# Feed-forward of a vision tower: the next chunk's first gatings ahead of the input's quantisation, products ahead of transposes, mean square on GpSimd

## The chip, the cores and the metric

The kernel runs on one core of one Trainium2 chip. The metric is the time of one execution in microseconds, as the device measures it. The engines are TensorE (PE; its weight loads are PEld), VectorE (DVE), ScalarE (ACT), GpSimd (POOL) and SyncE (SP), which issues DMAs.

## The reference, cut to what matters

A tower of an attention mixer, a gated linear attention, a mixture of experts, a linear attention over channels and, last, a quantised feed-forward on 4 x 3136 tokens of width 192. The change touches the feed-forward alone:

```python
def rmsnorm(x, g):
    return x * jax.lax.rsqrt(jnp.mean(x * x, axis=-1, keepdims=True) + EPS_NORM) * g

def activation_quant(x):
    scale = 127.0 / jnp.maximum(jnp.max(jnp.abs(x), axis=-1, keepdims=True), EPS_Q)
    return jnp.clip(jnp.round(x * scale), -128, 127) / scale

# bitlinear(x, w, g): x_norm = rmsnorm(x, g); quantise x_norm; multiply by w rounded to -1, 0, 1
h = bitlinear(x, w_in, g_in)          # 192 -> 2 x 512
up, gate = jnp.split(h, 2, axis=-1)
y = jax.nn.silu(gate) * up
return bitlinear(y, w_out, g_out)     # 512 -> 192
```

The result is added to the residual.

## The kernel before

The five phases follow one another. In the last one, `attention_and_ffn_phase` (L1651), the 12544 tokens are 28 chunks (`NC`) of 448, each four tiles (`TPC`, q = 0 to 3) of 112 tokens on the partitions. The channel attention runs over the chunks first; then the feed-forward runs over them again, with the channel attention's last map (`map_late`, `add_half`) mixed into its chunks g = 1 to 7. These are called early chunks here, the others middle chunks, apart from the last two.

There is no planner: each engine's program is written out in order, and semaphores (`F[...]`) join them. For chunk g of the feed-forward:

- VectorE: `weigh_in` (input times gain), `largest_in` (maximum), `quant_in` (L2482 to L2493: five small operations on 4 values a partition, each waiting for the one before, then four roundings and a conversion to bf16). `gated(g, q)` (L2501) makes y of tile q as silu times the up product times a scale. `mean_square` (L2506), `largest_y` (L2510, two tiles each), `quant_y` (L2525 to L2537, small operations and half of the rounding), `result` (L2547, output times scale plus residual).
- TensorE: `transpose_in` (L2035), `into(g, q)` (L2048: the gate and the up product of tile q), `transpose_y` (L2060), `outof(g, pair)` (L2081).
- ScalarE: `take_x` (L2224, PSUM to xT), `silu` (L2230), `squares` (L2240, the sum of y squared), `scaled_y` (L2247) and `whole_y` (L2253, the other half of the rounding and the conversion), `take_y` (L2259, PSUM to yT).
- GpSimd: `weigh` (L1872, yg = y times gain, one tile of 112 x 512 each), `root_of` (L1877, mean square to the power of -1/2).
- SyncE stores the chunk.

The loop is skewed: in turn g, chunk g's gatings stand with the input quantisation of chunk g + 1, the input weighing of chunk g + 2, and the output of chunk g - 1. Buffers limit it: y, yg5, xT and yT exist once, the products' PSUM banks and sg twice; `into(g, q)` waits until tile q - 2 is gated. `APART` = 8: input transposes up to chunk 8 share PSUM with those of y.

VectorE's turn g ends with `quant_y(g)`; the next operations in the trace, from L2482 on, are turn g + 1's `quant_in(g + 2)`.

Of the kernel before, what the change touches and what calls it, by code (L numbers as in the profile page):

```python
# [11 lines left out]
ALU = mybir.AluOpType  # L12
# [11 lines left out]
TPC = CH // T  # L24
CPI = TOK // CH
NC = B * CPI
# [17 lines left out]
HID = 256  # L44
# [1606 lines left out]
def attention_and_ffn_phase(nc, ins, h, bns, mean, rstd, var, minus, eye, rows_out, out):  # L1651

    HID = 512
# [7 lines left out]
    with ExitStack() as ctx:  # L1661
# [82 lines left out]
        ssq = sb("ssq5", [T, TPC])  # L1744
# [12 lines left out]
        def pga(g, q):  # L1757
# [9 lines left out]
        names5 = ("w_in", "gin_in", "set", "wc", "wsum_mm", "wsc_out", "ready", "xq_out", "xtr_mm", "xT_out", "in_mm", "up_mm",  # L1767
                  "sg_out", "y_out", "yg_out", "ssq_out", "r2_in", "r2_out", "yq_out", "ytr_mm", "yT_out", "o_mm",
                  "o_out", "stored", "dvec", "dvec2", "xg_out", "am_out", "fac_in", "fac_out", "scaled", "d2_out",
                  "xr_out", "yr_out", "s2_out", "ya_out")  # L1770
        F = {n: sem(f"{n}_5") for n in names5}
        out_t = out.rearrange("b (t p) d -> p (b t) d", p=T)
        first_in = [sem(f"first_in{i}_4") for i in range(4)]
# [31 lines left out]
        @block.gpsimd  # L1805
        def _(pool):
            for n, (buf, value) in enumerate(((eps5[:], 1e-5), (mhalf[:], -0.5), (xTB[RB:RB + 1], 1.0),
                                              (wl[64:128, 1, :].bitcast(F32), 0.0))):
                nc.gpsimd.memset(buf, value).then_inc(S["w_ready"], 1)
                pool.wait_ge(S["w_ready"], n + 1)  # L1810
            nc.gpsimd.memset(ones[:], 1.0).then_inc(F["set"], 1)
            pool.wait_ge(F["set"], 1)
            nc.gpsimd.memset(mhalf5[:], -0.5).then_inc(F["set"], 1)
            pool.wait_ge(F["set"], 2)

            def add_rows(g, k):

                if k:
                    pool.wait_ge(first_in[g % 4], 16 * (g // 4 + 1))
                else:  # L1820
                    pool.wait_ge(S["xa_out"], g + 1)
                r0 = k * NTOK + g * CH
                nc.gpsimd.dma_start(acc[g % 4], rows_out[r0:r0 + CH].rearrange("(q p) d -> p q d", p=T),
                                    accum_op=ALU.add).then_inc((first_in, both_in)[k][g % 4], 16)

            def add_bet(g):

                nc.gpsimd.dma_start(h[:, g * TPC:(g + 1) * TPC, :], bet.unsqueeze(1).broadcast_to([T, TPC, D]),
                                    accum_op=ALU.add).then_inc(bet_in[g % 4], 16)

            def factor(g):

                pool.wait_ge(S["agg_out"], g + 1)
                nc.gpsimd.tensor_tensor(veps[:], agg[:, :, 1], eps5[:], ALU.add).then_inc(S["veps_out"], 1)
                pool.wait_ge(S["veps_out"], g + 1)
                if g >= 1:
                    pool.wait_ge(S["nrm_out"], g)
                nc.gpsimd.tensor_tensor(rst[:], veps[:], mhalf[:], ALU.pow).then_inc(S["rst_out"], 1)

            def factor4(g):  # L1840

                pool.wait_ge(S["agg4_out"], g + 1)
                nc.gpsimd.tensor_tensor(veps4[:], agg4[:, :, 1], eps5[:], ALU.add).then_inc(S["veps4_out"], 1)
                pool.wait_ge(S["veps4_out"], g + 1)
                if g >= 1:
                    pool.wait_ge(S["xn_ready"], g)
                nc.gpsimd.tensor_tensor(rst4[:], veps4[:], mhalf[:], ALU.pow).then_inc(S["rst4_out"], 1)

            pool.wait_ge(S["e_in"], 32)
            for s in range(-LEAD, NC):  # L1850
                if here(s + 5):
                    add_rows(s + 5, 0)
                if here(s + 3):
                    factor(s + 3)
                if here(s + 5):
                    add_bet(s + 5)
                    add_rows(s + 5, 1)
                if here(s + 2):
                    factor4(s + 2)

            def factor5(n, cols):

                pool.wait_ge(F["fac_in"], min(n + 1, 2))
                nc.gpsimd.tensor_tensor(fac[:, cols], var[:, cols], mhalf5[:, cols], ALU.pow).then_inc(F["fac_out"], 1)

            def weigh(g, pair):

                for q in (2 * pair, 2 * pair + 1):
                    if g:
                        pool.wait_ge(F[("ya_out", "yr_out")[pair]], g)  # L1870
                    pool.wait_ge(F["y_out"], g * TPC + q + 1)
                    nc.gpsimd.tensor_tensor(yg5[:, q, :], y[:, q, :], gout[:], ALU.mult).then_inc(F["yg_out"], 1)  # L1872

            def root_of(g):

                pool.wait_ge(F["r2_in"], g + 1)
                nc.gpsimd.tensor_tensor(r2[:], ms2[:], mhalf5[:, 0:TPC], ALU.pow).then_inc(F["r2_out"], 1)  # L1877

            factor5(0, slice(0, HEAD))
            pool.wait_ge(F["gin_in"], 32)  # L1880
            for g in range(NC):
                weigh(g, 0)
                weigh(g, 1)
                root_of(g)
                if g in (AFTER, AFTER + 1):
                    half = HEAD + (g - AFTER) * (NT - HEAD) // 2
                    factor5(1 + g - AFTER, slice(half, half + (NT - HEAD) // 2))

        @block.tensor
        def _(pe):  # L1890
# [230 lines left out]
            into(1, 1)  # L2121
            for g in range(1, NC):
                late = NC - CPI + g - 1
                transpose_y(g - 1)
                if late < NC:
                    into(g, 2)
                    if g + 1 < NC:
                        transpose_in(g + 1)
                else:
                    if g + 1 < NC:  # L2130
                        transpose_in(g + 1)
                    into(g, 2)
                into(g, 3)
                if late < NC:
                    map_late(late, 0)
                outof(g - 1, 0)
                if late < NC:
                    map_late(late, 1)
                outof(g - 1, 1)
                if g + 1 < NC:  # L2140
                    enter(g + 1)
                    into(g + 1, 1)
# [5 lines left out]
        def _(act):  # L2148
# [116 lines left out]
            for g in range(NC):  # L2265
                if g:
                    scaled_y(g - 1)
                    whole_y(g - 1, 1)
                    whole_y(g - 1, 0)
                    take_y(g - 1)  # L2270
                squares(g, 0)
                silu(g, 2)
                squares(g, 1)
                silu(g, 3)
                squares(g, 2)
                squares(g, 3)
                if g + 1 < NC:
                    take_x(g + 1)
                    silu(g + 1, 0)
                    silu(g + 1, 1)  # L2280
# [6 lines left out]
        def _(dve):  # L2287
# [213 lines left out]
                nc.vector.scalar_tensor_tensor(y[:, q, :], pup[q % 2][0:T], dx[g % 2][:, q:q + 1], sg[q % 2 if g else 0],  # L2501
                                               ALU.mult, ALU.mult).then_inc(F["y_out"], 1)

            def mean_square(g):
                dve.wait_ge(F["ssq_out"], (g + 1) * TPC)
                nc.vector.tensor_scalar(ms2[:], ssq[:], 1.0 / HID, 1e-6, ALU.mult, ALU.add).then_inc(F["r2_in"], 1)  # L2506

            def largest_y(g, pair):
                dve.wait_ge(F["yg_out"], g * TPC + 2 * pair + 2)
                nc.vector.tensor_reduce(am2[:, 2 * pair:2 * pair + 2], yg5[:, 2 * pair:2 * pair + 2, :], AX.X, ALU.max,  # L2510
                                        apply_absolute_value=True)

            halves = [0]

# [3 lines left out]
                dve.wait_ge(F["dvec2"], halves[0])  # L2518

            def quant_y(g):  # L2520
                dve.wait_ge(F["r2_out"], g + 1)
                dve.wait_ge(F["r2_in"], g + 1)
                if g:
                    dve.wait_ge(F["ya_out"], g)
                link2(nc.vector.tensor_copy(s2[:], r2[:]))  # L2525
                link2(nc.vector.tensor_tensor(am2[:], am2[:], r2[:], ALU.mult))
                if g:
                    dve.wait_ge(F["o_out"], 2 * g)
# [81 lines left out]
            weigh_in(2)  # L2610
            gated(0, 3)
            largest_in(2)
            mean_square(0)
            largest_y(0, 1)
            quant_y(0)
            for g in range(1, NC):
                late = NC - CPI + g - 1
                if g + 1 < NC:
                    quant_in(g + 1)
                if g + 2 < NC:  # L2620
                    weigh_in(g + 2)
                gated(g, 0)
                gated(g, 1)
                if g + 2 < NC:
                    largest_in(g + 2)
                gated(g, 2)
                largest_y(g, 0)
                gated(g, 3)
                if late < NC:
                    add_half(late, 0, 0)  # L2630
                if late == NC:
                    dve.wait_ge(S["h_out"], 2 * NC + 2)
                    stats_of(NT - 2)
                result(g - 1, 0)
                mean_square(g)
                largest_y(g, 1)
                if late < NC:
                    add_half(late, 1, 0)
                result(g - 1, 1)
                quant_y(g)  # L2640
                if g == AFTER:
                    finish(1, slice(HEAD, NT))
# [112 lines left out]
```

## Time and profile before

| | us |
|---|---|
| median of 3 runs (2669.01 to 2669.86) | 2669.02 |
| the profiled execution's own time | 2666.92 |
| its span | 2665.1 |

The page, its head and the busy lines by slice:

```profile
span 2665.1 us, 45416 instructions
...
DVE  5777777777774688888872566664558778889896
ACT  2444444444443688888861676663778764667776
POOL 1100100100000167667673577676555533353433
PEclk9999999999998899999985999996779998777777
```

Each digit is one fortieth of the span, in tenths. The feed-forward is the last seven of them.

### The profile page before, as it was taken

The page shows a single profiled execution, that of the slowest core. Times are in us where ns is not written, and L with a number is a line of the kernel's source. Part 1 is how long each engine was busy: PE and PEld are TensorE (multiplying, and loading weights), DVE is VectorE, ACT ScalarE, POOL GpSimd, SP SyncE. Part 2 cuts the span into 40 slices and gives each one's busy share as a digit, 9 for nine tenths or more (in the row PEclk, how much of TensorE's full clock was granted, in tenths as well). Part 3 has the DMA queues.
Part 4 walks back from the last instruction along what each step waited for, and adds up shares of the span by engine and source line. Part 5 has one row for each costly group of instructions (what it writes and reads, how often), then busy time and mean ns, then how long its engine had stood idle before and what let it go on. Part 6 is the DMA issues. An engine that isn't in the chain of part 4 may idle for free. (4 is left out here: it accounts for less than half of the span.)

```text
span 2665.1 us, 45416 instructions
## 1 busy us (share of the span) xinstructions
PE 2250.9 (84%) x14046; PEld 1626.4 (61%) x14047; DVE 1924.3 (72%) x5417; ACT 1594.4 (60%) x2815; POOL 1040.1 (39%) x1101
## 2 busy tenths in 40 slices
PE   8999999999997899999982999991778887766655
PEld 4444444444443788888871999991667775544443
DVE  5777777777774688888872566664558778889896
ACT  2444444444443688888861676663778764667776
POOL 1100100100000167667673577676555533353433
PEclk9999999999998899999985999996779998777777
DMA  2000000000000333233235677777756720000000
GB/s 59 0 19 13 0 18 13 1 9 1 0 0 23 87 66 75 67 73 76 66 71 165 219 242 240 246 242 133 94 71 87 91 30 6 22 22 26 22 27 26
DMA packets 114522, 183.08 MB, mean 69 GB/s; under 512 B 14337, under 2 KB 84326, under 8 KB 114078
## 3 DMA queue, kind: packets, MB, share of 16 engines
q0 software_dynamic: 74816, 86.34, 17.3%
q1 hardware_dynamic: 39554, 94.84, 11.1%
q8 instruction: 80, 1.31, 0.2%
q14 instruction: 72, 0.59, 0.1%
HBM read 64.44 MB, written 64.39 MB: 48 GB/s over the span
## 5 line engine op out<-in xcount | busy, mean ns | idle before, releaser
L213 ACT ACTIVATE prob<-pscore 128x896 f32<-128x896 f32 x336 | 308.1, 917 | 423.5 <-PE pscore L295 423.5
L420 DVE TENSOR_REDUCE pmax<-ppre 112x1 f32<-112x512 f32 x656 | 424.3, 686 | 162.0 <-PE ppre L262 161.9
L309 PE MATMUL pout<-prob,xkey 128*64 128x448 f32 x1344 | 328.0, 567 | 0.4 <-ACT prob L213 0.4
L1578 POOL DMA_INDIRECT rows_out<-yb,home3b x252 | 244.5, 970 | 141.8 <-issue 59.3
L262 PE MATMUL ppre<-xh,yh 49*112 49x512 f32 x656 | 291.3, 446 | 7.8 <-DVE pmax L420 4.1
L195 POOL CAST yh<-ynext 113x448 fp32r<-113x448 f32 x28 | 17.2, 616 | 667.3 <-DVE pmax L420 639.2
L737 POOL DMA_INDIRECT rows_in<-xr,idx x224 | 235.1, 1050 | 76.3 <-issue 44.8
L262 PEld LDWEIGHTS ppre<-xh,yh 49*112 49x112 f32 x656 | 112.6, 172 | 239.5 <-issue 103.5
L295 PE MATMUL pscore<-yh,xh 49*128 49x448 f32 x700 | 241.2, 422 | 0.4 <-DVE yh L440 0.4
L1872 POOL TENSOR_TENSOR sums<-rows,gout 112x512 f32<-112x512 f32 x112 | 141.2, 1270 | 253.2 <-DVE rows L2501 253.2
L295 PE MATMUL pscore<-yh,xl 49*128 49x448 f32 x700 | 202.9, 364 | 0.0
L295 PE MATMUL pscore<-yl,xh 49*128 49x448 f32 x700 | 142.8, 364 | 0.0
L2060 PE MATMUL ptr<-eyeb,wT 112*128 112x112 bf16 x448 | 45.3, 292 | 114.1 <-ACT wT L2253 114.1
L1485 PE MATMUL pz<-xth3b,wd 128*128 128x448 f32 x504 | 140.7, 381 | 0.0
L1500 PE MATMUL py<-uph,zl 128*112 x504 | 131.8, 261 | 0.0
L1500 PE MATMUL py<-upl,zh 128*112 x504 | 131.6, 261 | 0.0
L1500 PE MATMUL py<-uph,zh 128*112 x504 | 131.5, 261 | 0.0
L309 PEld LDWEIGHTS pout<-prob,xkey 128*64 128x64 f32 x1344 | 66.6, 135 | 105.7 <-issue 85.3
L295 PEld LDWEIGHTS pscore<-yh,xl 49*128 49x128 f32 x700 | 127.9, 187 | 0.8
L1935 PE MATMUL pqk<-xh,wh 128*128 128x448 f32 x168 | 72.1, 429 | 56.4 <-ACT spent L2196 55.8
L2060 PEld LDWEIGHTS ptr<-eyeb,wT 112*128 112x128 bf16 x448 | 38.9, 141 | 126.8 <-ACT wT L2253 88.9
L1472 PE MATMUL ptr3b<-eye,xb 112*128 112x112 f32 x504 | 63.5, 271 | 61.9 <-DMA xb<-rows_in 42.8
(393 smaller groups left out, 6647.2 us busy)
## 6 DMA issues: line engine op xcount, KB each, us to landing
wd<-down SPq DMA_DIRECT2D x63, 512.0 KB
xb<-rows_in SPq DMA_DIRECT2D x63, 455.0 KB
sums<-rows_out POOLq DMA_DIRECT2D x56, 336.0 KB, 6.1
h<-brow POOLq DMA_DIRECT2D x28, 336.0 KB, 5.2
h<-gambet POOLq DMA_DIRECT2D x28, 336.0 KB, 4.9
out<-sums SPq DMA_DIRECT2D x28, 336.0 KB, 2.8
rows_in<-zero SPq DMA_DIRECT2D x15, 455.0 KB, 5.5
rows_out<-yb,home3b POOLq DMA_INDIRECT x252
```

The lines of the kernel that those rows point to most:

```text
L213: nc.scalar.activation(prob[j % 3][:, :, :], pscore[j % 2][:, :, 0:CH], ACT.Exp).then_inc(exped, 1)
L262: pe.matmul(out[:, :], yh1[rows, q * T:(q + 1) * T], xh[b % 2][rows, block * 512:(block + 1) * 512], start=True, stop=True, tile_position= ...
L295: mm = pe.matmul(pscore[j % 2][:, i, 0:CH], x[b % 2][rows, keys], y[rows], start=(n == 0), stop=(n == 2), tile_position=(i * LO, 0))
L309: mm = pe.matmul(pout[i * LO:(i + 1) * LO, 0:CH], xkey[b % 2][:, 2 * j + i, :], prob[j % 3][:, i, :], start=(j == 0), stop=(i == 1 and j = ...
L420: nc.vector.reduce_max(pmax[:, q, 2 * block + half:2 * block + half + 1], bank(u, depth), AX.X).then_inc(pre_max, 1)
L737: nc.gpsimd.indirect_dma_start(rows_in, bass.IndirectOffsetOnAxis(ap=idx[r % G3][:, 2 * q + k:2 * q + k + 1], axis=0), xr[r % G3][:, q, :] ...
L1485: mm = pe.matmul(pz[m][:, 0:CH], wd[i][:, w, cols], x, start=(s_ == 0), stop=(s_ == 4))
L1500: mm = pe.matmul(py[i][:, q // 2, (q % 2) * D:(q % 2 + 1) * D], zz[i][m][:, cols], w[:, bass.ds(2 * e + m, 1), :], start=(m + n == 0), sto ...
L1578: nc.gpsimd.indirect_dma_start(rows_out, bass.IndirectOffsetOnAxis(ap=home[r][:, q:q + 1], axis=0), yb[r % 2][:, q, :], None).then_inc(ret ...
L1872: nc.gpsimd.tensor_tensor(yg5[:, q, :], y[:, q, :], gout[:], ALU.mult).then_inc(F["yg_out"], 1)
L1935: mm = pe.matmul(pqk[m % 2][:, 0:CH], w, x, start=(n == 0), stop=(n == 4))
L2060: mm = pe.transpose(pyt[:, half, k * CH + q * T:k * CH + (q + 1) * T], yq[:, q, (2 * half + k) * 128:(2 * half + k + 1) * 128], eyeb[0:T, ...
```

## The change

Five things, all in the feed-forward's loops over g:

- VectorE: `gated(g, 0)` and `gated(g, 1)` stand at the head of the turn, ahead of `quant_in(g + 1)` and `weigh_in(g + 2)`.
- TensorE: `into(g, 2)` and `into(g, 3)` stand ahead of `transpose_y(g - 1)` and `transpose_in(g + 1)`.
- ScalarE: the silus of tiles 2 and 3 and the squares of tiles 0 and 1 stand ahead of `take_y(g - 1)`; each silu stands ahead of its square.
- The mean square moves from VectorE to GpSimd, ahead of the power in `root_of`.
- `quant_y` loses its copy of r2 to s2; a semaphore `am2_out` takes over its ordering.

```diff
@@ root_of (GpSimd)
+                if g:
+                    pool.wait_ge(F["s2_out"], g)
+                pool.wait_ge(F["ssq_out"], (g + 1) * TPC)
+                nc.gpsimd.tensor_scalar(ms2[:], ssq[:], 1.0 / HID, 1e-6, ALU.mult, ALU.add).then_inc(F["r2_in"], 1)
                 pool.wait_ge(F["r2_in"], g + 1)
@@ TensorE's loop
+                into(g, 2)
+                into(g, 3)
                 transpose_y(g - 1)
-                if late < NC:
-                    into(g, 2)
-                    if g + 1 < NC:
-                        transpose_in(g + 1)
-                else:
-                    if g + 1 < NC:
-                        transpose_in(g + 1)
-                    into(g, 2)
-                into(g, 3)
+                if g + 1 < NC:
+                    transpose_in(g + 1)
@@ ScalarE's loop
+                silu(g, 2)
+                squares(g, 0)
+                silu(g, 3)
+                squares(g, 1)
+                if g:
                     take_y(g - 1)
-                squares(g, 0)
-                silu(g, 2)
-                squares(g, 1)
-                silu(g, 3)
@@ VectorE
-            def mean_square(g):
-                dve.wait_ge(F["ssq_out"], (g + 1) * TPC)
-                nc.vector.tensor_scalar(ms2[:], ssq[:], 1.0 / HID, 1e-6, ALU.mult, ALU.add).then_inc(F["r2_in"], 1)
@@ largest_y
-                                        apply_absolute_value=True)
+                                        apply_absolute_value=True).then_inc(F["am2_out"], 1)
@@ quant_y
+                dve.wait_ge(F["am2_out"], 2 * g + 2)
                 dve.wait_ge(F["r2_out"], g + 1)
-                dve.wait_ge(F["r2_in"], g + 1)
-                link2(nc.vector.tensor_copy(s2[:], r2[:]))
@@ VectorE's loop
+                gated(g, 0)
+                gated(g, 1)
                 if g + 1 < NC:
                     quant_in(g + 1)
                 if g + 2 < NC:
                     weigh_in(g + 2)
-                gated(g, 0)
-                gated(g, 1)
```

## Rows read from the trace of the kernel before

**Rows 1.** The page, busy us of each engine.

```profile
PE 2250.9 (84%) x14046; PEld 1626.4 (61%) x14047; DVE 1924.3 (72%) x5417; ACT 1594.4 (60%) x2815; POOL 1040.1 (39%) x1101
```

**Rows 2.** Windows: stretch, its length, busy PE, PEld, DVE, ACT, POOL, granted clock, DMA.

```profile
2249.60:2353.72 104.12, 74.53 (x433) 55.98 (x432) 88.33 (x241) 65.84 (x115) 36.28 (x30) 0.77 0.07 21
...
2399.83:2620.21 220.38, 139.90 (x837) 95.53 (x836) 197.85 (x511) 164.42 (x284) 90.72 (x75) 0.75 0.09 24
```

**Rows 3.** VectorE's waits (us, times, longest), 2249.60 to 2353.72, then from 2620.21.

```profile
DVE rows L2501 <- PE pg L2048: 7.6, 12, 0.7
DVE h L2346 <- PE po L1947: 6.1, 6, 1.6
...
DVE rows L2501 <- ACT sg L2230: 5.1, 1, 5.1
DVE rows L2501 <- PE pg L2048: 3.8, 1, 3.8
```

**Rows 4.** Timeline of VectorE in a middle chunk: start us, us, operation [idle before].

```profile
2446.10 0.15 DVE L2482 TENSOR_TENSOR am<-am,fac 112x4 f32<-112x4 f32 x1
...
2448.56 1.40 DVE L2464 SCALAR_TENSOR_TENSOR xg<-h,mean,gin 112x192 f32<-112x192 f32 x4
...
2449.87 0.75 DVE L2501 SCALAR_TENSOR_TENSOR rows<-pg,dx,sg 112x512 f32<-112x512 f32 x1
...
2451.19 0.94 DVE L2470 TENSOR_REDUCE am<-xg 112x4 f32<-112x768 f32 x1
...
2452.92 0.75 DVE L2501 SCALAR_TENSOR_TENSOR rows<-pg,dx,sg 112x512 f32<-112x512 f32 x1 [0.78 <-PE pg L2048]
...
2454.71 0.74 DVE L2501 SCALAR_TENSOR_TENSOR rows<-pg,dx,wqp 112x512 f32<-112x512 f32 x1
...
2456.30 0.59 DVE L2506 TENSOR_SCALAR ms<-ssq 112x4 f32<-112x4 f32 x1 [0.20 <-ACT spent L2240]
2456.90 1.22 DVE L2510 TENSOR_REDUCE am<-sums 112x2 f32<-112x1024 f32 x1
...
2458.68 0.16 DVE L2525 COPY s<-r 112x4 f32<-112x4 f32 x1
...
2460.62 0.15 DVE L2482 TENSOR_TENSOR am<-am,fac 112x4 f32<-112x4 f32 x1
```

**Rows 5.** Timeline of GpSimd in the same chunk; last, a small operation at 2187.96.

```profile
2450.76 2.50 POOL L1872 TENSOR_TENSOR sums<-rows,gout 112x512 f32<-112x512 f32 x2 [7.31 <-DVE rows L2501]
...
2455.60 1.27 POOL L1872 TENSOR_TENSOR sums<-rows,gout 112x512 f32<-112x512 f32 x1 [0.50 <-DVE rows L2501]
...
2456.97 1.01 POOL L1877 TENSOR_TENSOR r<-ms,mhalf 112x4 f32<-112x4 f32 x1
...
2187.96 0.20 POOL L1843 TENSOR_TENSOR veps<-agg,eps 112x4 f32<-112x4 f32 x1 [9.61 <-DVE agg L2319]
```

**Rows 6.** The mean square's shortest, median, longest (ns); timeline near the start.

```profile
L2506 DVE TENSOR_SCALAR ms<-ssq x28: 160/589/594, 2231.1 to 2647.4; 112x4 f32<-112x4 f32 x28
...
15.14 1.88 DVE L480 TENSOR_TENSOR xl<-x,xh 113x1664 fp32r<-113x1664 f32 x1
15.37 2.07 POOL L195 CAST yh<-ynext 113x448 fp32r<-113x448 f32 x1 [12.14 <-DVE ynext L414]
```

**Rows 7.** Timeline of ScalarE and TensorE in the same middle chunk.

```profile
2446.54 1.99 ACT L2253 ACTIVATE wT<-xn 112x1024 bf16<-112x1024 f32 x2
...
2449.55 1.71 ACT L2259 COPY maps<-ptr 128x896 bf16<-128x896 bf16 x2 [1.02 <-PE ptr L2060]
...
2452.51 1.06 PE L2048 MATMUL pqk<-winq,xT 96*112 96x512 bf16 x2
...
2458.02 0.59 PE L2048 MATMUL pqk<-winq,xT 96*112 96x512 bf16 x2
...
2458.65 0.69 ACT L2230 ACTIVATE wqp<-pqk,dx 112x512 f32<-112x512 f32 x1 [0.17 <-PE pqk L2048]
```

More of the change, by code:

```diff
@@ L1769, in attention_and_ffn_phase @@
                   "o_out", "stored", "dvec", "dvec2", "xg_out", "am_out", "fac_in", "fac_out", "scaled", "d2_out",
-                  "xr_out", "yr_out", "s2_out", "ya_out")
+                  "xr_out", "yr_out", "s2_out", "ya_out", "am2_out")
         F = {n: sem(f"{n}_5") for n in names5}
@@ L2612, in _ @@
             largest_in(2)
-            mean_square(0)
             largest_y(0, 1)
@@ L2634, in _ @@
                 result(g - 1, 0)
-                mean_square(g)
                 largest_y(g, 1)
```

## The prediction

> **What bounds the kernel now.** The change touches only the last stage, the quantised feed-forward, so I read that stage and leave the rest of the span at its time. The page's busy list gives VectorE as the second busiest engine of the whole span [rows 1]; the windows over the stage show more: in the fifteen middle chunks (g = 11 to 25) VectorE is busy 197.85 of 220.38 us, TensorE 139.90, ScalarE 164.42, GpSimd 90.72, at a granted clock of 0.75 of full, a mix of the 2.4 and 1.2 GHz levels [rows 2]. VectorE sets the pace: a chunk takes 220.38 / 15 = 14.69 us, and only what stands in VectorE's own order, or makes it wait, counts. The waits view says what it waits for: TensorE's products (7.6 us in 12 waits and 6.1 us in 6 over the six early chunks g = 2 to 7, and 3.8 and 5.1 us once each in the last two) [rows 3].
>
> Then one middle chunk on VectorE in order of time [rows 4]. Zero is the input's quantisation at 2446.10. It lasts 2.46 us (to 2448.56), the weighing of the input 1.31 (to 2449.87), the first two gatings together 1.32 (to 2451.19). After the maximum of the input, VectorE waits 0.78 for the third tile's product. The fourth gating starts at 2454.71; the result ends near 2456.10, the mean square sits there until 2456.89, and the second maximum starts at 2456.90. The chunk closes at 2460.62: 14.52 us. One chunk in three takes about 15.3, which makes the mean 14.69.
>
> **The row that decides.** The mean square is a tensor_scalar on four elements a partition; alone it takes 0.16 us, its median is 0.589 [rows 6]. In this chunk it starts at 2456.30 and ends at 2456.89; GpSimd's multiplication of the fourth tile runs from 2455.60 for 1.27, to 2456.87 [rows 4, 5]. The small operation ends 0.02 after the multiplication does: it was held by it. The opposite direction shows once, early on: a VectorE tensor_tensor with two SBUF inputs runs from 15.14 for 1.88, and a GpSimd cast that starts at 15.37 takes 2.07 [rows 6]. Gating, which reads PSUM and one SBUF tile, isn't held: it starts at 2452.92 within the pair of multiplications of 2450.76 to 2453.26 and takes its usual 0.75 [rows 4, 5].
>
> The Trainium skill states this as a rule (SBUF — State Buffer, section "SBUF: two separate sides"): VectorE operations in a two-port mode or with two SBUF inputs, and GpSimd operations, take one shared port pair as an exclusive lock for the whole instruction. It speaks against this change. By it the quantisation's first operation, a tensor_tensor on two SBUF inputs, is held too, which no row here shows in that direction; if only its tensor_scalar operations were held, the sum would be 0.2 us a chunk lower.
>
> **The change on VectorE, step by step.** New zero: the start of gated(g,0), right after quant_y(g-1).
>
> 1. gated(g,0) and gated(g,1) come first: 1.32 us. Their inputs are there: the second silu of the next chunk starts at 2458.65 and ends at 2459.34, and the gatings come at 2460.4 at the earliest [rows 7]. This costs nothing by itself. But GpSimd's two multiplications now start 0.89 after the first gating (2450.76 against 2449.87) and last 2.50, from 0.89 to 3.39 [rows 4, 5]. Before, the quantisation was over by then. Now it is due at 1.32, and its one tensor_tensor and its tensor_scalars meet them. If one small operation slips in between the two multiplications, the rest starts at about 3.4 and ends at 5.53; if none does, at 5.72; without the hold it would end at 3.78. Hold: 1.75 to 1.94, taken as 1.84. This is the dearest term.
> 2. The third and fourth products are issued as soon as gated(g,0) and gated(g,1) are done, so on TensorE they are finished before 4.5 even at the half clock (a pair of matmuls 1.06 there, 0.59 at full [rows 7]). The third gating is due after 7. The wait of 0.78 goes.
> 3. The copy to s2 goes: 0.16 and a handoff, 0.20 [rows 4].
> 4. The mean square leaves VectorE. Its slot (2456.10 to 2456.90) is 0.80. But the second maximum reads the fourth weighed tile, ready 0.89 + 1.27 + 0.03 = 2.19 after the fourth gating starts, and VectorE has 1.39 of work until then. So a wait of 0.80 takes the slot's place: gain nil.
> 5. On GpSimd the mean square costs 0.20 if it is like the small tensor_tensor [rows 5], and comes after the fourth multiplication; with the power of 1.01 behind it, r2 is ready some 1.35 after the second maximum starts, and quant_y needs it after 1.78 (2456.90 to 2458.68) [rows 4, 5]. Hidden. From both sides: nothing, or, at the price of a power (1.0), a wait of 0.4 a chunk, 10 us in all; I take nothing, by the nearest row in size.
> 6. ScalarE puts two silus and two squares ahead of the copies of yT. Rounding ends 2.43 after zero (2446.54 + 1.99); two silus and two squares, 1.3 a pair, follow, so the copies (1.71 for two), with the transposes behind the third and fourth products, end near 7.4 instead of 5.2, and the first output product near 8.3 [rows 7]. The result that needs it stands behind the weighing, a maximum, two gatings and another maximum, near 10. Hidden in middle chunks, by the very hold of step 1. The input's transposes wait for the quantised input at 5.5 to 5.7; they come before that product and are over by 6.7.
>
> Middle chunk: 14.52 - 0.78 - 0.20 - 0.80 + 0.80 + 1.84 = 15.38, against a mean of 14.69: +0.69. For fifteen chunks +10.3. Chunks 8 to 10 take 2399.83 - 2353.72 = 46.11 [rows 2] with extra work in it; I give them +0.5 each, +1.5.
>
> 7. Early chunks 2 to 7: 104.12 us [rows 2], with 13.7 us of waits for products [rows 3] that the earlier issue and the longer chunk clear, and 6 x 0.3 for the copy and a mean square of 0.16. The hold adds 6 x 1.84 = 11.0. VectorE's additions to the residual, which stand between the fourth gating and the second maximum here, fill the time of the fourth multiplication, so no wait of step 4 comes in. -13.7 - 1.8 + 11.0 = -4.5. Chunk 1, which overlaps the stage's start: half of an early chunk's share, -0.4.
> 8. The last two chunks [rows 3]: waits of 3.8 and 5.1 go, and 0.4 of copies; the hold comes once (+1.84); new waits for silu and for yT, whose copies are now behind two silus (from step 6, near 0.5 in chunk 26, and 1.85 and 1.9 in chunk 27), add 4.2; -8.9 - 0.4 + 1.8 + 4.2 = -3.3.
> 9. The clock. After the output product TensorE makes the next chunk's first two tiles, and ScalarE turns to quant_y's scaling only after their silus. In the chunk shown the second silu ends 4.63 after the fourth gating starts; the scaling is due at 4.9 (2.19 to the second maximum, 1.78 to quant_y, 0.9 of its small operations) [rows 4, 7]: slack 0.25, where the weighing of the next input used to cover 3.8 more. At 1.2 GHz three product groups add 3 x 0.47 = 1.4. Scaling is then 1.15 late, GpSimd's multiplications (0.5 of slack) about 0.65, and they hold the quantisation that much later: +0.5. If it stays one chunk in three, six of eighteen: +3.
>
> Sum: +10.3 + 1.5 - 4.5 - 0.4 - 3.3 + 3.0 = +6.6 us. The profiled span was 2665.1, in a run of 2666.92; the median of the three runs is 2669.02, 3.9 over the span. Forecast: span 2671.7, time 2675.6. The changed order takes VectorE's waits for products away and pays with the port.
>
> **Rivals.**
> *A: VectorE keeps the port once it has it.* It gets in between the two multiplications, and the second waits for the quantisation instead. The hold is 0.7 (1.32 to 2.02), 1.1 less in 26 chunks: -29 on the sum, 2646. For it: the GpSimd cast of rows 6 did wait for VectorE. Against: that was one long operation; the quantisation is a chain with a handoff after each operation, where GpSimd can step in. It ends faster than before, on the other side of the forecast, and decides as soon as the hold is under 1.5 us a chunk.
> *B: no hold at all*, because the mean square's 0.589 is peculiar to its place. 26 x 1.84 = 48 less, 2628. Against: its length goes from 0.160 to 0.594 with nothing of its own changed, and in the chunk shown it ends with the multiplication [rows 4 to 6].
> *C: the clock falls.* TensorE's stretches of work get shorter, with new gaps before the transposes and the output product. If all middle and early chunks see step 9's price: 18 more chunks x 0.5 = +9, 2685. Against: the clock's mean is 0.75 to 0.77 over the stage already, with the long gap before the transposes of y in it [rows 2].
>
> **From these to the numbers.** Forecast 0.67, A 0.15, B 0.05, C 0.13. The forecast's own range is 2665 to 2685: the hold's bounds (+-2.5), the early chunks (+-3), the last two (+-1.5), the clock (0 to +6), part of step 5's upper bound. To hold 8 in 10 I take in C and reach towards A: 2650 to 2690. A measurement of this kernel tells 0.2%, 5.3 us, from no change. The forecast lies at +0.25%: of its 0.67 I give 0.37 to slower, 0.27 to no change, 0.03 to faster. With the rivals: slower 0.50, same 0.27, faster 0.23.
>
> **What the changed profile would show.** Right: the quantisation's first or second operation over 1 us long, ending with a GpSimd multiplication; no wait for products ahead of the third gating; a wait of about 0.8 for GpSimd ahead of the second maximum; middle chunks of 15.3 to 15.6 us, early ones near 16.6, the last two together near 26. Wrong: small operations of the quantisation all at 0.16 to 0.23 us, chunks near 13.5 (B); GpSimd's second multiplication over 3 us with chunks near 14.3 (A); a granted clock under 0.65 in the middle chunks (C); quant_y waiting for r2 (step 5).

## The result, and the profile after

| | before | after |
|---|---|---|
| median, us | 2669.02 (5 runs, 2665.63 to 2669.86) | 2681.07 (5 runs, 2679.11 to 2684.56) |
| profiled execution: own time, span | 2666.92, 2665.1 | 2679.11, 2677.3 |
| mean granted clock | 0.912 | 0.898 |

The ratio is 1.0047, with an interval of 1.0033 to 1.0061: slower, by 12.05 us between the medians and 12.5 by the ratio. The forecast said slower by 6.6, and its range held the result. Nearly all of the loss is where it was placed, in the middle chunks. The head and the busy lines of the page after answer to [rows 1]:

```profile
span 2677.3 us, 45417 instructions
PE 2278.8 (85%) x14046; PEld 1641.0 (61%) x14047; DVE 1956.8 (73%) x5361; ACT 1586.6 (59%) x2815; POOL 1043.0 (39%) x1129
...
PEclk9999999999998899999985999995788997876666
```

VectorE has 56 instructions fewer (28 copies, 28 mean squares) and is busy 32.5 us longer. The last four slices of the clock stand at 6, where before they stood at 7. GpSimd has 28 instructions more.

The windows over the same chunks as [rows 2] (stretch, its length, busy PE, PEld, DVE, ACT, POOL, granted clock, DMA): chunks 2 to 7, then 11 to 25.

```profile
2250.70:2352.17 101.47, 73.23 (x433) 56.25 (x432) 97.46 (x229) 64.72 (x115) 37.40 (x36) 0.82 0.08 21
...
2400.24:2634.35 234.11, 161.36 (x841) 102.09 (x840) 215.68 (x481) 160.35 (x286) 93.38 (x90) 0.65 0.08 23
```

A middle chunk takes 234.11 / 15 = 15.61 us, where it took 14.69. VectorE's busy time in it is 14.38 instead of 13.19 (+1.19), its idle time 1.23 instead of 1.50 (-0.27). So the change did win idle time, and lost four times as much in busy time, although it took two small operations off VectorE. In the early chunks the sum goes the other way: busy 97.46 instead of 88.33 (+9.1), idle 4.0 instead of 15.8 (-11.8).

One middle chunk, VectorE, ScalarE and GpSimd in order of time (start, us, operation [idle before]); it answers to [rows 4, 5]:

```profile
2448.73 0.69 ACT L2229 ACTIVATE wqp<-pqk,dx 112x512 f32<-112x512 f32 x1 [1.02 <-PE pqk L2052]
2448.86 0.75 DVE L2501 SCALAR_TENSOR_TENSOR rows<-pg,dx,sg 112x512 f32<-112x512 f32 x1
2449.32 1.32 ACT L2246 ACTIVATE xn<-sums,s 112x512 f32<-112x512 f32 x2
...
2449.75 0.75 DVE L2501 SCALAR_TENSOR_TENSOR rows<-pg,dx,wqp 112x512 f32<-112x512 f32 x1
2450.42 0.15 DVE L2482 TENSOR_TENSOR am<-am,fac 112x4 f32<-112x4 f32 x1
...
2450.60 0.17 DVE L2483 TENSOR_SCALAR am<-am 112x4 f32<-112x4 f32 x1
2450.71 2.49 POOL L1872 TENSOR_TENSOR sums<-rows,gout 112x512 f32<-112x512 f32 x2 [4.04 <-ACT xn L2246]
2450.81 1.20 DVE L2484 TENSOR_SCALAR dx<-am,wsc 112x4 f32<-112x4 f32 x1
...
2451.92 0.17 DVE L2485 RECIPROCAL sx<-am 112x4 f32<-112x4 f32 x1
2452.12 1.10 DVE L2486 TENSOR_TENSOR sx<-sx,fac 112x4 f32<-112x4 f32 x1
...
2457.08 0.74 DVE L2501 SCALAR_TENSOR_TENSOR rows<-pg,dx,sg 112x512 f32<-112x512 f32 x1
...
2461.05 1.22 DVE L2506 TENSOR_REDUCE am<-sums 112x2 f32<-112x1024 f32 x1 [0.79 <-POOL sums L1872]
2461.11 0.19 POOL L1879 TENSOR_SCALAR ms<-ssq 112x4 f32<-112x4 f32 x1
2461.38 1.01 POOL L1881 TENSOR_TENSOR r<-ms,mhalf 112x4 f32<-112x4 f32 x1
...
2462.84 0.15 DVE L2521 TENSOR_TENSOR am<-am,r 112x4 f32<-112x4 f32 x1
```

To be seen here: GpSimd's two multiplications stand from 2450.71 to 2453.20. Two operations of four values a partition, started inside them, take 1.20 and 1.10 us; the first ends with the first multiplication (2450.71 + 1.25 = 2451.96, against 2452.01), the second with the second (2453.22). Alone the same lines take 0.23 and 0.16. The third gating, at 2457.08, has no wait ahead of it, the second maximum has its 0.79, and the mean square and the power on GpSimd end at 2462.39, before quant_y asks for them. GpSimd itself waited 4.04 us, the last of it for ScalarE's scaling.

It is so in every middle chunk: two operations are held in each. In twelve of the fifteen they are the two shown; in the other three they are the second of these (1.04) and the first of the four roundings behind it (1.29 instead of 0.31). The operations by line over chunks 11 to 25 (shortest, median, longest in ns):

```profile
L2484 DVE TENSOR_SCALAR dx<-am,wsc x15: 229/1196/1215, 2403.9 to 2622.3; 112x4 f32<-112x4 f32 x15
L2486 DVE TENSOR_TENSOR sx<-sx,fac x15: 1042/1103/1110, 2405.2 to 2623.6; 112x4 f32<-112x4 f32 x15
```

The waits of the same stretch (us, times, longest):

```profile
POOL sums L1872 <- ACT xn L2246: 59.8, 15, 4.0
DVE am L2506 <- POOL sums L1872: 11.9, 15, 0.8
```

Fifteen waits for the fourth weighed tile, of 0.8; fifteen of GpSimd that end with the scaling; none of VectorE for a product. One wait for a product is too short to be listed there: in nine of the fifteen chunks the second gating starts about 0.2 later than in the other six, each time 0.21 after the end of the product that it reads. The first line is this product in the chunk shown; it ends at 2449.54, and the gating starts at 2449.75. The other two are from the next chunk, where the product takes 0.84 and the gating follows the first one without a gap:

```profile
2448.48 1.06 PE L2052 MATMUL pg<-winq,xT 96*112 96x512 bf16 x2
...
2464.20 0.84 PE L2052 MATMUL pg<-winq,xT 96*112 96x512 bf16 x2
2465.26 0.75 DVE L2501 SCALAR_TENSOR_TENSOR rows<-pg,dx,wqp 112x512 f32<-112x512 f32 x1
```

The nine chunks take 15.70 or 15.71 us, the six 15.40 to 15.51.

### The profile page after: what moved, and what is told of

The parts are those of the page before. It is cut to its first block and busy times, and to the rows that moved or that the text cites. A ratio compares the mean times of both kernels' runs of the same rounds, so it can differ in the third digit from the quotient of the medians.

```text
span 2677.3 us, 45417 instructions
## 1 busy us (share of the span) xinstructions
PE 2278.8 (85%) x14046; PEld 1641.0 (61%) x14047; DVE 1956.8 (73%) x5361; ACT 1586.6 (59%) x2815; POOL 1043.0 (39%) x1129
## 5 line engine op out<-in xcount | busy, mean ns | idle before, releaser
L2085 PE MATMUL po<-woutq,maps 128*112 128x192 bf16 x448 | 73.1, 333 | 70.3 <-DVE sums L2542 48.4
L2052 PE MATMUL pqk<-winq,xT 96*112 96x512 bf16 x224 | 100.1, 542 | 24.7 <-DVE rows L2501 19.2
```

The source lines that it names most:

```text
L2052: mm = pe.matmul(dst[0:T], xT[:, c, q * T:(q + 1) * T], winq[:, c, o:o + HID], start=(c == 0), stop=(c == 1))
L2085: mm = pe.matmul(po[0:T, 1, i * D:(i + 1) * D], yT[:, k, q * T:(q + 1) * T], woutq[:, k, :], start=(k == 0), stop=(k == 3), skip_group_che ...
```

## The experiments

Six of the eight kernels start from the kernel after, two (vec_order_only and mean_square_only) from the kernel before. The next table gathers what they gave; the ratio is to the kernel before, whose median beside them was 2669.02 (the kernel after), 2666.08 (the first four experiments) and 2666.47 (the last four). Chunk is the mean of chunks 11 to 25, from the first operation of quant_y to the next. Busy is VectorE's share of the window from 2400 to 2600 times the chunk, idle the rest, clock the granted clock of that window.

| kernel | median | ratio (interval) | chunk | busy | idle | clock |
|---|---|---|---|---|---|---|
| before | | | 14.69 | 13.17 | 1.52 | 0.75 |
| after | 2681.07 | 1.0047 (1.0033 to 1.0061) | 15.61 | 14.42 | 1.19 | 0.65 |
| short_mul | 2641.74 | 0.9900 (0.9880 to 0.9920) | 13.99 | 12.58 | 1.41 | 0.65 |
| vec_order_only | 2696.37 | 1.0101 (1.0080 to 1.0122) | 16.52 | 15.04 | 1.48 | 0.67 |
| vec_order_undone | 2716.09 | 1.0185 (1.0159 to 1.0211) | 16.44 | 12.50 | 3.94 | 0.70 |
| mean_square_only | 2664.54 | 0.9995 (0.9978 to 1.0011) | 14.58 | 12.43 | 2.15 | 0.75 |
| mul_after_weighing | 2659.93 | 0.9971 (0.9950 to 0.9992) | 14.76 | 12.53 | 2.23 | 0.66 |
| late_mul | 2644.82 | 0.9922 (0.9892 to 0.9952) | 14.31 | 12.70 | 1.61 | 0.67 |
| scaling_first | 2673.10 | 1.0024 (1.0007 to 1.0041) | 15.31 | 13.65 | 1.66 | 0.65 |
| late_mul_scaling | 2650.61 | 0.9944 (0.9919 to 0.9969) | 14.34 | 12.60 | 1.74 | 0.66 |

### short_mul: is it GpSimd's multiplication that holds?

```diff
-                    nc.gpsimd.tensor_tensor(yg5[:, q, :], y[:, q, :], gout[:], ALU.mult)
+                    cols = slice(0, 64 if g and pair == 0 else HID)
+                    nc.gpsimd.tensor_tensor(yg5[:, q, cols], y[:, q, cols], gout[:, cols], ALU.mult)
```

> The changed kernel, but GpSimd weighs only 64 of 512 columns of tiles 0 and 1 from chunk 1 on (the rest of their yg is left out). Everything else, the order on every engine too, stays. If the port held by these two multiplications is the cause, the quantisation's small operations fall from over 1 us to 0.2 to 0.5, a middle chunk from 15.61 to about 14.1, and the time to 2640 to 2655. Rival: TensorE's lower clock and ScalarE's new order set the chunk, and the hold only fills a wait that would be there anyway: then the waits for products and for yT grow by what the hold loses, and the time stays above 2672.

The kernel leaves 448 of 512 columns of two tiles unweighed, so it is a probe and not a kernel to use.

Measured: 2641.74, a chunk of 13.99. The operation that stood at 1.20 is back at its own length; by line over the middle chunks:

```profile
L2485 DVE TENSOR_SCALAR dx<-am,wsc x15: 229/250/252, 2404.4 to 2600.0; 112x4 f32<-112x4 f32 x15
```

No engine's order is changed, the granted clock is the same 0.65 as after, and the chunk is 1.62 us shorter: 1.84 less busy, 0.22 more idle. Waits for the output product come up where the kernel after has none (7.6 us in 11 waits from 2400 to 2610). The hold is the cause of the loss, and the low clock doesn't keep the kernel from being 1% faster than before; what the clock costs this run doesn't measure.

### vec_order_only and vec_order_undone: one half of the reordering each

vec_order_only is the kernel before with the two gatings at the head of VectorE's turn; vec_order_undone is the kernel after with this same edit taken back.

```diff
+                gated(g, 0)
+                gated(g, 1)
                 if g + 1 < NC:
                     quant_in(g + 1)
                 if g + 2 < NC:
                     weigh_in(g + 2)
-                gated(g, 0)
-                gated(g, 1)
```

> The kernel before, with only VectorE's order changed (first two gatings ahead of the input's quantisation and weighing). The hold theory puts the whole loss here: hold of 1.8 to 1.9 us a chunk, the wait of 0.78 for the third product mostly covered by it, copy and mean square still on VectorE: a middle chunk of 15.6 to 15.8, time 2680 to 2690. Rival (the loss comes from TensorE's and ScalarE's order and the clock): 2669 or less.

Measured: 2696.37, a chunk of 16.52. The hold came as expected, in ten of the fifteen chunks on the first two operations:

```profile
L2482 DVE TENSOR_TENSOR am<-am,fac x13: 149/853/859, 2404.9 to 2603.2; 112x4 f32<-112x4 f32 x13
L2483 DVE TENSOR_SCALAR am<-am x13: 169/1193/1266, 2405.8 to 2604.1; 112x4 f32<-112x4 f32 x13
```

Busy time rose by 1.87 a chunk and idle time stayed (1.48 against 1.52), so it came out slower than expected. The waits from 2400 to 2610 say why the waits for products stayed:

```profile
PE po L2035 <- DVE gambet L2493: 17.8, 13, 2.2
...
DVE rows L2501 <- PE pg L2048: 8.9, 14, 0.7
```

TensorE has the input's transposes ahead of the third product in this order, these need the quantised input, and that is now both later and held. The earlier gatings could release the product, but it wasn't next in TensorE's order. That these transposes are what keeps the waits is read from the rows; no run moved them alone.

> The changed kernel with VectorE's old order (quantisation and weighing of the input first), all else as changed. No hold by the hold theory: quantisation operations at 0.15 to 0.23 us. The third and fourth products now stand ahead of the transposes of y while their buffers come free only 4.5 us into the chunk, so the transposes and the output product come late, and a wait of about 1 us for the output product takes the place of the one of 0.78 for the third: chunk 14.3 to 15.0, time 2660 to 2678. Rival (TensorE's and ScalarE's order is the cause): 2681 or more.

Measured: 2716.09, a chunk of 16.44. This was a miss: it is the slowest of all, and its time lies where the rival (TensorE's and ScalarE's order is the cause) had put it. The hold is gone (busy 12.50, the lowest but one), and idle time has grown to 3.94. VectorE from the fourth gating to the result of one chunk (start, us, [idle before]), then its waits from 2400 to 2610:

```profile
2511.13 0.74 DVE L2501 SCALAR_TENSOR_TENSOR rows<-pg,dx,wqp 112x512 f32<-112x512 f32 x1
2515.11 0.74 DVE L2542 SCALAR_TENSOR_TENSOR sums<-po,d,h 112x192 f32<-112x192 f32 x2 [3.24 <-PE po L2085]
...
DVE sums L2542 <- PE po L2085: 38.1, 19, 3.2
```

I had expected a wait of at most 1 us for the output product. It is 3.2: with products, silus and squares ahead of the transposes and copies of the previous y, and the gatings that release those products back behind quantisation and weighing, that whole chain ends 3.2 too late. The rival is right that this order costs much under VectorE's old one. Under VectorE's new one it isn't the cause of the loss: short_mul keeps it and is faster than before, and so do mul_after_weighing and late_mul below, which leave no work out. So their new order needs VectorE's, and by vec_order_only VectorE's needs theirs. Alone they cost 30 us (VectorE's) and 50 us (theirs), together 12.

### mean_square_only: the slot on VectorE against the wait for the fourth tile

The kernel before, with the mean square on GpSimd ahead of the power, the copy gone, and `am2_out` ordering quant_y: the last two of the five items of the change.

> The kernel before, with only the mean square moved to GpSimd and the copy of r2 dropped. By the prediction the mean square's slot of 0.8 us turns into a wait of 0.8 for the fourth weighed tile, and only the copy's 0.20 is gained: 27 x 0.2 = 5 us, 2664. Rival (the slot's 0.59 is gained too): 2650. Second rival (r2 comes late, a power's price for the small operation): 2675.

Measured: 2664.54, ratio 0.9995 with 1 inside the interval, a chunk of 14.58 (-0.11). VectorE's waits from 2400 to 2610:

```profile
DVE rows L2505 <- PE pg L2052: 13.3, 13, 2.0
DVE am L2510 <- POOL sums L1872: 9.6, 14, 0.8
```

Busy -0.74, idle +0.63: the slot turned into a wait ahead of the second maximum, and the product waits are what they were. At most the copy was won: a chunk is 0.11 shorter and the copy was worth 0.20, while the time shows no difference from before.

### mul_after_weighing and late_mul: keep the work, end the collision

In mul_after_weighing GpSimd starts on tiles 0 and 1 once VectorE has weighed the next input. late_mul also puts the fourth gating ahead of the first maximum.

```diff
@@ weigh(g, pair) (GpSimd), in both
+                if pair == 0 and 1 <= g < NC - 2:
+                    pool.wait_ge(F["xg_out"], g + 3)
@@ VectorE's loop, late_mul alone
                 gated(g, 2)
-                largest_y(g, 0)
                 gated(g, 3)
+                largest_y(g, 0)
```

> The changed kernel, but GpSimd's multiplications of tiles 0 and 1 wait until VectorE has quantised and weighed the input (chunks 1 to 25). No work is left out. By the hold theory every quantisation operation falls back to 0.15 to 0.23 us (1.9 us a chunk gone), and new waits take part of its place: the first maximum waits about 1 us for the second weighed tile. Middle chunk 15.61 to about 15.2, time 2668 to 2676. Rival (the port isn't it, the clock or ScalarE's order is): the quantisation keeps its long operations or the chunk grows by the delay, 2690 or more.

Measured: 2659.93, ratio 0.9971, more of a gain than expected; the terms that the expectation names, 1.9 off and 1 on, give a chunk of 14.7 and not the 15.2 written there. By line the operation is at 229 ns again, and the price is a wait of about 1 us ahead of the first maximum (GpSimd's row and VectorE's maximum of one chunk):

```profile
L2486 DVE TENSOR_SCALAR dx<-am,wsc x14: 228/230/231, 2411.1 to 2603.2; 112x4 f32<-112x4 f32 x14
...
2473.74 3.72 POOL L1874 TENSOR_TENSOR sums<-rows,gout 112x512 f32<-112x512 f32 x3 [7.67 <-DVE xg L2466]
...
2476.27 1.22 DVE L2508 TENSOR_REDUCE am<-sums 112x2 f32<-112x1024 f32 x1 [0.96 <-POOL sums L1874]
```

Against after: busy -1.89, idle +1.04, chunk -0.85. The busy time is the hold, and it measures it once more at 1.9.

> As mul_after_weighing, and the fourth gating also stands ahead of the first maximum, so that GpSimd's four multiplications follow one another beside gatings and maxima, which don't take the port. Worked out from the rows: input quantised at 3.8 and weighed at 5.1 after the first gating, fourth weighed tile at 10.2, second maximum to 11.4, chunk 13.8. If the hold was the only thing that kept the changed order from gaining, the time is 2635 to 2650, below both kernels. Rival: TensorE and ScalarE bound the chunk once the hold is gone; then waits for the output product and for silu appear and the time stays above 2655.

Measured: 2644.82, ratio 0.9922 (0.9892 to 0.9952), the fastest kernel that computes everything, 0.8% below the kernel before. The chunk is 14.31, half a microsecond over the expectation. One chunk, VectorE and GpSimd:

```profile
2482.17 4.95 POOL L1874 TENSOR_TENSOR sums<-rows,gout 112x512 f32<-112x512 f32 x4 [7.95 <-DVE xg L2466]
2483.00 0.74 DVE L2503 SCALAR_TENSOR_TENSOR rows<-pg,dx,sg 112x512 f32<-112x512 f32 x1
2483.66 0.74 DVE L2503 SCALAR_TENSOR_TENSOR rows<-pg,dx,wqp 112x512 f32<-112x512 f32 x1
2484.70 1.22 DVE L2508 TENSOR_REDUCE am<-sums 112x2 f32<-112x1024 f32 x1 [0.30 <-POOL sums L1874]
```

All four multiplications now run in one row of 4.95 us beside gatings and maxima, which they don't lengthen. What kept it from the expected time are small waits for GpSimd (0.3 to 0.6, 8.4 us in 23 waits from 2390 to 2600) and for the output product (5.2 us in 17).

### scaling_first and late_mul_scaling: is GpSimd late because of ScalarE's order?

ScalarE's second silu of the next chunk goes behind the scaling in scaling_first; late_mul_scaling has this and late_mul's edits.

```diff
                     scaled_y(g - 1)
+                    silu(g, 1)
                     whole_y(g - 1, 1)
@@ end of the turn
                     silu(g + 1, 0)
-                    silu(g + 1, 1)
```

> The changed kernel, but ScalarE's scaling of y (two operations) stands ahead of the next chunk's second silu. In the changed kernel's trace GpSimd waited for this scaling 22 times. By step 9 of the prediction the multiplications start 0.2 to 0.9 us earlier, the hold falls on the quantisation's first operations, and a middle chunk takes 15.3 to 15.45 instead of 15.61: 2673 to 2678. Rival (only where the hold falls changes, not its length, and the silu now comes late for the second gating): 2680 to 2686.

Measured: 2673.10, ratio 1.0024, a chunk of 15.31, that is 0.30 less than after; the intervals of the two ratios overlap, so the gain rests on the chunks. GpSimd's waits for the scaling are gone, and its multiplications start 0.89 after the first gating. The hold meets the quantisation's first operations instead (0.27 and 1.21, by line):

```profile
L2482 DVE TENSOR_TENSOR am<-am,fac x14: 266/271/277, 2406.8 to 2605.8; 112x4 f32<-112x4 f32 x14
L2483 DVE TENSOR_SCALAR am<-am x14: 1208/1214/1220, 2407.1 to 2606.1; 112x4 f32<-112x4 f32 x14
```

These two are 0.12 + 1.04 = 1.16 over their own lengths, 0.75 less than after, and a new wait of 0.5 for the second silu ahead of the second gating (6.4 us in 13 waits from 2400 to 2600) takes most of that back. The two hang together: while VectorE waits for the silu, the first multiplication passes. So ScalarE's order is a cause of GpSimd's lateness, but 0.30 is the balance of two effects and not the price of the lateness.

> late_mul and scaling_first together. With the multiplications waiting for the weighing, the scaling is no longer waited for by GpSimd; it only starts the rounding of y, its transposes and the output product earlier by up to 0.9 us at the low clock. If the output product is what VectorE waits for in late_mul, this gains 0.2 to 0.5 us a chunk over it; if not, it is the same or loses up to 0.4 a chunk by the later silu.

Measured: 2650.61, ratio 0.9944, a chunk of 14.34. No gain on late_mul's 14.31: where GpSimd's multiplications wait for the weighing anyway, the scaling isn't what starts them, and the silu's wait of 0.5 (6.9 us in 14) stays. Its median lies 5.8 us above late_mul's; in the profiled executions it is the early chunks that are slower (2 to 7: 98.55 against 91.61).

## Why the prediction was right, and where it was off

The time is 5.5 us above the forecast of 2675.6 and 3.9 below rival C's 2685. The spans differ by +12.2 us. By stretches, from the first operation of quant_y on:

| | forecast | measured |
|---|---|---|
| ahead of the first of these | 0 | +1.1 |
| chunk 1 | -0.4 | 0.0 (16.84 both) |
| chunks 2 to 7 | -4.5 | -2.7 (104.12 to 101.47) |
| chunks 8 to 10 | +1.5 and 0.5 of the clock's term | +2.0 (46.11 to 48.07) |
| chunks 11 to 25 | +10.3 and 2.5 of the clock's term | +13.7 (220.38 to 234.11) |
| last two | -3.3 | -1.8 (29.59 to 27.83) |
| behind them | 0 | -0.2 |

What was missed is nearly all on the slow side (+1.1, +0.4, +1.8, +0.9 and +1.5), so it isn't errors cancelling that kept the result in the range.

- **Step 1, the hold, right.** Forecast 1.84, measured 0.97 + 0.94 = 1.91 in the chunk shown (1.20 instead of 0.23, 1.10 instead of 0.16). It was read off a single operation [rows 6]. short_mul and mul_after_weighing showed the cause and its size. "This costs nothing by itself" was wrong by a little: in nine of fifteen chunks the second gating waits 0.20 for its product, at the low clock. This is the rule of the Trainium skill (SBUF — State Buffer, section "SBUF: two separate sides"), and the tensor_tensor on two SBUF inputs, which no row of before could show in this direction, is held as it says: 1.10 for 0.16. For a GpSimd power these traces don't bear it out (last section). The multiplications started not 0.89 but 1.85 after the first gating, which is step 9's doing. Where they do start at 0.89, in ten middle chunks of vec_order_only, the hold is 0.71 + 1.03 = 1.74 (0.86 instead of 0.15, 1.20 instead of 0.17), the lower of the two bounds.
- **Steps 2 and 3, right.** No wait for the third tile's product is left in the middle chunks. vec_order_only adds what the step didn't say: that needs TensorE's order too.
- **Step 4, right:** 0.79 for a slot of 0.80, and mean_square_only measured the pair as nothing.
- **Step 5, right.** 0.19 for the mean square; r2 is ready 1.34 after the second maximum starts (forecast 1.35), and quant_y comes at 1.79.
- **Step 6, right, and a narrow thing.** The first output product starts at 2456.64 and the result needs it at 2459.53. It is hidden by the order on VectorE: vec_order_undone, which takes this order away, lays 3.2 of it bare. That the hold does part of the hiding, as the step has it, fits the waits for this product that come back where it is gone (7.6 us in 11 in short_mul, 5.2 in 17 in late_mul).
- **Step 7, the waits mis-sized.** Idle time fell by 11.8, not by 13.7; about 1 us of waits for the residual's product and 0.8 for the output product are left. That is the 1.8 that the early chunks lack.
- **Step 8, mis-sized.** The new waits of the two chunks come to 7.0 us, not 4.2 (3.9 in four for the output product, 2.7 and 0.4 in one each). About 1.6 of that comes back: the mean square's slot of 0.8 goes in both chunks, and no wait for GpSimd takes its place. The largest, ahead of the third gating of chunk 27, is 2.73, not 1.85: the silu behind the rounding ends at 2654.58, and the gating starts at 2654.71. The profile names GpSimd for it, whose multiplication ends at 2654.68, but by the program the gating waits for this silu and for nothing of GpSimd's that is so late. ScalarE was itself 0.9 later than forecast, for step 9's reason.
- **Step 9, the mechanism right, its spread wrong.** In the chunk shown quant_y's scale is ready at 2448.03 and the scaling starts at 2449.32, behind the silu: 1.3 late, forecast 1.15. But I gave it to one chunk in three, at 0.5, and it is in all fifteen, at less. The one in three was misread too: of the fifteen middle chunks of before only three take 15.3 (13, 16 and 19). In place of 0.5, by rows: the late start lengthens the hold from 1.74 (vec_order_only's chunks) to 1.91, that is 0.17, and the second gating's late product makes nine of fifteen chunks 0.26 longer, 0.16 in the mean. With 1.74 in the forecast's sum a chunk is 15.28, and 15.28 + 0.17 + 0.16 = 15.61, the mean measured. This is an estimate from rows of two kernels. scaling_first's 15.31 comes near steps 1 to 5's 15.38 by chance: its hold is 1.16 and it waits 0.5 for a silu.

**The rivals.** A is refuted for the quantisation: a VectorE operation does slip in between the two multiplications, but it holds the second up by nothing that shows (2.49 for the two, as in [rows 5]), and the next one is held in its turn. What A builds on does happen with longer operations (last section). B is refuted by every row above. C was half there. The granted clock of the middle chunks did fall, 0.75 to 0.65, on the very line that was drawn for it, after a change that put new gaps between TensorE's stretches of work; in the early chunks it rose, 0.77 to 0.82, against C. It spread over all fifteen middle chunks, as C had it, but its price was below C's 0.5 a chunk: at most about 0.33 by the rows of step 9. It doesn't decide the loss: short_mul and late_mul run at 0.65 and 0.67 and are faster than before. Why the clock fell isn't shown. All kernels with the gatings at the head of VectorE's turn stand at 0.65 to 0.67, the others at 0.70 to 0.75; that the gaps between TensorE's stretches did it is argued, no run varied them alone.

**What stays open.** The 1.1 us ahead of the first quant_y were not traced to a cause; over the profiled executions of all ten kernels this point lies between 2230.0 and 2238.4, so 1.1 need not come from the change. Why the second product runs wholly at the low clock in nine middle chunks and not in the other six is open too.

## What to carry to other kernels

A reordering on the critical engine is to be laid over the timeline of the engine it shares a port with: here two operations of 0.2 us on four values cost 1.9 us more together, each chunk, because they fell under a neighbour's long one, and moving the neighbour under work that isn't held (gating from PSUM, maxima) turned a loss of 0.5% into a gain of 0.8%. A small operation whose median is several times its shortest, as the mean square's 589 ns against 160, is where to look for such a hold before a change makes it worse. Orders on several engines that release each other are to be changed and judged together: the halves of this one cost 30 and 50 us, the whole 12.

## What was unexpected of the hardware

Not every VectorE operation is held. In the next chunk GpSimd's multiplications start at 2466.43. A reciprocal from SBUF to SBUF starts 0.03 later and keeps its length, then the tensor_tensor behind it takes the hold, and the first of the four roundings takes it again:

```profile
2466.43 2.49 POOL L1872 TENSOR_TENSOR sums<-rows,gout 112x512 f32<-112x512 f32 x2 [4.04 <-ACT xn L2246]
2466.46 0.17 DVE L2485 RECIPROCAL sx<-am 112x4 f32<-112x4 f32 x1
2466.67 1.04 DVE L2486 TENSOR_TENSOR sx<-sx,fac 112x4 f32<-112x4 f32 x1
2467.75 1.97 DVE L2488 TENSOR_SCALAR rows<-xg,sx 112x192 f32<-112x192 f32 x4
```

The reciprocal is a weak sign, since it may have gone in before the port was taken. The maximum at 2457.74 (1.21) and the gating of 2458.87 (0.74) are better ones: they keep their lengths under the multiplication of 2457.97 to 2459.24. The input's weighing, which reads two SBUF tiles, doesn't; in chunk 9, two tiles of it:

```profile
2375.04 2.81 POOL L1872 TENSOR_TENSOR sums<-rows,gout 112x512 f32<-112x512 f32 x2
2375.31 2.76 DVE L2464 SCALAR_TENSOR_TENSOR xg<-h,mean,gin 112x192 f32<-112x192 f32 x2
```

Two tiles of the weighing take 0.7 where four take 1.40 (from one middle chunk of before, [rows 4]). Here GpSimd is held as well: its two multiplications take 2.81 and not 2.49. And between two multiplications that GpSimd runs back to back, a waiting VectorE operation gets in: the hold of the chunk shown first is two holds of 0.97 and 0.94, with a reciprocal and a handoff between them, and not one of 2.4.

Nor does every GpSimd operation hold. One of its powers runs in the kernel before over the quantisation and the weighing. The operation that the change lengthened to 1.10 keeps its 0.16, and the weighing, with two SBUF inputs in each of four tiles, its 1.40 (timeline of chunk 9):

```profile
2371.48 4.17 POOL L1864 TENSOR_TENSOR fac<-var,mhalf 112x24 f32<-112x24 f32 x1 [4.07 <-DVE var L2456]
...
2372.18 0.16 DVE L2486 TENSOR_TENSOR sx<-sx,fac 112x4 f32<-112x4 f32 x1
...
2373.89 1.40 DVE L2464 SCALAR_TENSOR_TENSOR xg<-h,mean,gin 112x192 f32<-112x192 f32 x4
```
